# A decoder layer with a mixture of experts: expert rows in five tiles of 128 and one odd row, two groups per expert

## The reference

```
N, E, F = 4096 tokens, 8 experts, 512
capacity = int(N / E * 1.25) + 1                 # 641 rows for an expert
scores = softmax(xf @ wg); top1 = argmax(scores); combine_w = scores[top1]
rank = position of the token among those of its expert
slot = top1 * capacity + rank  (rank < capacity, else dropped)
eb = rows of xf by slot, 8 x 641 x 128           # empty slots are zero
y = gelu(eb @ W1 + b1) @ W2 + b2                 # 128 -> 512 -> 128
out = y[slot] * combine_w  (0 for a dropped token)
x = layernorm(x + out)
```

## Time and profile before

| what | value |
|---|---|
| time, median of 3 runs | 502.6 us (502.14 to 502.91) |
| profiled execution: its own time, and its span | 500.05 us, 498.1 us |
| busy in the span: PE, PEld, DVE, ACT, POOL | 88%, 61%, 68%, 58%, 58% |
| last work of the attention stage | about 381.7 us into the span |
| second layer of expert 0 starts; of expert 7 | 399.06 us; 472.16 us |

### The profile page before, as it was taken

How to read it: one execution, slowest core, us unless ns; L and a number is a source line. 1 busy time by engine, 2 the same in 40 slices (tenths; PEclk the granted TensorE clock), 3 DMA queues, 4 the chain that set the end, 5 groups by cost and what they waited for, 6 DMA issues and landing times.

```text
span 498.1 us, 18035 instructions
## 1 busy us (share of the span) xinstructions
PE 438.9 (88%) x6359; PEld 304.1 (61%) x6359; DVE 337.2 (68%) x1672; ACT 286.8 (58%) x627; POOL 290.7 (58%) x518
## 2 busy tenths in 40 slices
PE   3689999999999999999999999999861699999930
PEld 2355666666666666666666666666540488888730
DVE  5165677777787787777777777777774267767730
ACT  1256566766666776666676765676542256667620
POOL 5344555566566566566656666656444036887883
PEclk9999999999999999999999999999985599999985
DMA  4600000000111000011000010000004333344100
GB/s 148 227 13 12 24 14 17 24 25 24 29 34 30 24 24 24 25 35 33 25 24 24 24 37 17 19 13 19 15 29 120 84 81 89 101 107 128 26 19 18
DMA packets 30891, 22.51 MB, mean 45 GB/s; under 512 B 4460, under 2 KB 27281, under 8 KB 30804
## 3 DMA queue, kind: packets, MB, share of 16 engines
q1 hardware_dynamic: 27604, 17.16, 12.2%
q0 software_dynamic: 3200, 4.22, 2.8%
HBM read 12.25 MB, written 9.65 MB: 44 GB/s over the span
## 4 chain that ended last, share of the span: by engine, by line
PE 69%; issue 14%; POOL 9%; DMA 2%; DVE 1%; ACT 1%; SPq 1%; POOLq 1%; DVEq 0%; ACTq 0%
PE banks L529 14%; PE banks L591 13%; PE banks L537 9%; PE banks L545 8%; PE banks L523 6%; POOL out_x L480 6%; PE banks L602 6%; PE banks L670 3%; PE banks L618 3%; POOL rs L470 2%; PE banks L682 2%; PE banks L736 1%; PE banks L571 1%; PE banks L573 1%; PE banks L572 1%
## 5 line engine op out<-in xcount | busy, mean ns | idle before, releaser
L1001 DVE TENSOR_REDUCE mx<-banks 128x8 f32<-128x1024 f32 x64 | 75.4, 1219 | 12.4 <-PE banks L545 12.3
L417 POOL TENSOR_SCALAR QE<-qT,head_mask 128x128 f32<-128x128 f32 x128 | 75.6, 607 | 9.9 <-DVE qT L917 9.9
L806 ACT ACTIVATE arena<-banks 128x1024 f32<-128x1024 f32 x64 | 62.1, 1022 | 20.8 <-PE banks L545 20.8
L771 ACT ACTIVATE arena<-banks 128x1024 f32<-128x1024 f32 x64 | 62.1, 1023 | 18.0 <-PE banks L545 15.6
L591 PE MATMUL banks<-arena,V 128*32 128x128 f32 x2048 | 69.9, 276 | 1.2 <-ACT arena L806 0.7
L423 POOL TENSOR_TENSOR rs<-ve,minus_half 128x1 f32<-128x1 f32 x32 | 17.7, 552 | 84.4 <-DVE ve L971 84.4
L591 PEld LDWEIGHTS banks<-arena,V 128*32 128x32 f32 x2048 | 51.7, 109 | 12.6 <-issue 9.7
L480 POOL DMA_INDIRECT out_x<-ot,idx x48 | 49.9, 1040 | 12.1 <-issue 10.2
L434 POOL TENSOR_TENSOR rs<-ve,minus_half 128x1 f32<-128x1 f32 x32 | 18.1, 566 | 49.5 <-DVE ve L990 49.5
L818 ACT COPY yx<-banks 128x512 f32<-128x512 f32 x32 | 18.8, 586 | 48.9 <-PE banks L591 48.9
L545 PE MATMUL banks<-later,identb 64*64 64x256 bf16 (+1 forms) x448 | 46.3, 299 | 0.0
(11 more groups left out here) (150 smaller groups left out, 1004.7 us busy)
## 6 DMA issues: line engine op xcount, KB each, us to landing
w_sb<-in_L_ffn_W SPq DMA_DIRECT2D x16, 256.0 KB
expert_in<-zeros SPq DMA_DIRECT2D x10, 273.0 KB, 3.2
EB<-expert_in SPq DMA_DIRECT2D x8, 341.2 KB
X<-in_x SPq DMA_DIRECT2D x32, 64.0 KB, 1.8
C<-in_ctx SPq DMA_DIRECT2D x32, 64.0 KB, 1.9
out_x<-fb SPq DMA_DIRECT2D x32, 64.0 KB
out_x<-ot,idx POOLq DMA_INDIRECT x48
b2b<-in_L_ffn_b SPq DMA_DIRECT2D x1, 512.0 KB, 5.2
```

Of the source, the lines that this page charges most:

```text
L417: last = g.tensor_scalar(QE[b % 2][:, a, :], qT[b % 2][:], head_mask[:, a:a + 1], None, ALU.mult)
L771: nc.scalar.activation(A1[b % 2][:, 2 * half:2 * half + 2].rearrange("p j a t -> p j (a t)"), pair("s1", half), ACT.Relu).then_inc(s1_out[ ...
L806: nc.scalar.activation(P2[b % 2][:, 2 * half:2 * half + 2].rearrange("p j a t -> p j (a t)"), pair("s2t", half), ACT.Exp, scale=SCALE).the ...
L1001: v.tensor_reduce(mx[b % 2][:, 8 * half:8 * half + 8].rearrange("p (j a) -> p j a", a=NA), pair("s2", half).rearrange("p j (a t) -> p j a ...
```

## The change

The rows of an expert are five tiles of 128 (640 rows) and one odd row, the 641st. `ET` becomes 5, `CAPP` 656, and `JT = ET + 1` counts the tiles with the odd one. An expert's load now gives each partition five consecutive rows of the buffer (2600 bytes) where it gave six rows 112 apart (520 bytes each). The eight odd rows come with one small load (`ER`, 8 rows) and are transposed together once; each expert's hidden layer treats its odd row as column 641. In the second layer the odd row goes first: four matmuls with W2 as weights and one column moving. VectorE copies that column into `restY`; during expert 7 the eight columns are transposed back and finished as one tile of 8 rows. Each expert has two groups, tiles 0 to 2 and 3 to 4. `shifted` of the first group stands after `summed` of tile 4, that of the second after the next expert's `gated` and `token_rows`.

```diff
+    ET = CAP // P
+    JT = ET + 1
+    ROWS = ET * P + 1
+    HALVES = [(0, 321), (321, ROWS)]
+    CAPP = 656
...
+        GROUPS = [(e, tiles) for e in range(E) for tiles in ([0, 1, 2], [3, 4])]
...
             def expert_rows(e):
-                sp.dma_start(EB[e % 3][:], buf[e * CAPP:(e + 1) * CAPP, :].rearrange("(c p) d -> p c d", p=ER)).then_inc(
+                sp.dma_start(EB[e % 3][:], buf[e * CAPP:e * CAPP + ET * P, :].rearrange("(p c) d -> p c d", c=ET)).then_inc(
                     eb_in[e % 3], 16)
...
+            expert_rows(0)
+            sp.dma_start(ER[:], buf.rearrange("(e c) d -> e c d", c=CAPP)[:, ET * P, :]).then_inc(er_in, 16)
+            for e in range(1, 3):
                 expert_rows(e)
```

On GpSimd:

```diff
-            for n in range(GROUPS):
-                root(n)
-                if n >= LATE:
-                    scatter(n - LATE)
-            for n in range(GROUPS - LATE, GROUPS):
-                scatter(n)
+            for e in range(E):
+                if e > 0:
+                    scatter(2 * e - 1)
+                root(2 * e)
+                if e == E - 1:
+                    root_rest()
+                root(2 * e + 1)
+                scatter(2 * e)
+            scatter_rest()
+            scatter(2 * E - 1)
```

On TensorE, in `second_layer`:

```diff
-                for c in range(ET):
-                    n, rows = e * ET + c, tile_rows(c)
-                    if n >= 2:
-                        pe.wait_ge(y_done, n - 1)
+                for k in range(JT):
+                    i = e * JT + k
+                    if i >= 2:
+                        pe.wait_ge(y_done, i - 1)
                     for f in range(FC):
-                        mm = pe.matmul(max_bank[n % 2][0:rows, 0:D], hT[e % 2][:, f, c * ER:c * ER + rows],
-                                       w2_sb[e % 2][:, f, :], start=(f == 0), stop=(f == FC - 1))
+                        if k == 0:
+                            mm = pe.matmul(max_bank[i % 2][:, 0:1], w2_sb[e % 2][:, f, :], hT[e % 2][:, f, ET * P:ROWS],
+                                           start=(f == 0), stop=(f == FC - 1))
+                        else:
+                            mm = pe.matmul(max_bank[i % 2][:, 0:D], hT[e % 2][:, f, (k - 1) * P:k * P],
+                                           w2_sb[e % 2][:, f, :], start=(f == 0), stop=(f == FC - 1))
                     mm.then_inc(y_full, 1)
+                    if e == E - 1 and k == 2:
+                        pe.wait_ge(t_done, 2 * E)
+                        pe.transpose(dve_bank[0][0:E, 0:P], restY[:], ident[:]).then_inc(rest_full, 1)
```

On ScalarE, after the eight Gelus of expert e:

```diff
-                for n in range(max(0, (e - 1) * PER + 1), e * PER + 1):
-                    scaled(n)
+                if e > 0:
+                    scaled(2 * e - 1)
+                scaled(2 * e)
```

On VectorE:

```diff
+            for e in range(E):
+                if e > 0:
+                    spread_of(e - 1, ET - 1, stats(e - 1, ET - 1))
+                gate_mark = gated(e)
+                token_rows(e)
+                if e == 0:
+                    rest_mark = rest_gated()
                 else:
+                    shifted(2 * e - 1)
+                if e + 1 < E:
+                    rows_turned(e + 1)
+                rest_copied(e)
+                for c in range(ET):
+                    if c > 0:
+                        mark = stats(e, c - 1)
+                    summed(e, c, gate_mark)
+                    if c > 0:
+                        spread_of(e, c - 1, mark)
+                    if c == ET - 1:
+                        shifted(2 * e)
+                if e == E - 1:
+                    spread_of(e, ET - 1, stats(e, ET - 1))
+                    rest_summed(rest_mark)
+            dve.wait_ge(rstd_rest, 1)
...
```

More of the change, by code:

```diff
@@ L1 @@
+import math
 from contextlib import ExitStack
@@ L199, in decoder, with late @@
         w2_sb = ring("w2_sb", 2, [P, FC, D])
[L200 to L210, removed]
+        EB = ring("EB", 3, [P, ET, DR])
+        ER = sb("odd_rows", [E, DR])
+        b2r = sb("b2r", [E, D])
+        def late(at, shape):
+            size = math.prod(shape)
+            assert at + 2 * size <= 4 * SC
+            parts = [arena[:, at + k * size:at + (k + 1) * size] for k in range(2)]
+            if len(shape) == 2:
+                parts = [part.rearrange("p (a b) -> p a b", a=shape[0]) for part in parts]
+            return parts, at + 2 * size
+        ebT, end = late(0, [ROWS])
+        hT, end = late(end, [FC, ROWS])
+        xg, end = late(end, [ET, D])
         act_bank = [banks[:, k, :] for k in range(4)]
@@ L362, in _ @@
             for k in range(4):
-                sp.wait_ge(out_done[k], 16 * GT * (GROUPS // 4))
+                sp.wait_ge(out_done[k], 16 * sum(len(GROUPS[n][1]) for n in range(k, len(GROUPS), 4)))
+            sp.wait_ge(rest_out, 16)
         @block.gpsimd
@@ L465, in root @@
             def root(n):
-                e, c = n // PER, n % PER * GT
+                e, tiles = GROUPS[n]
+                c0, c1 = tiles[0], tiles[-1] + 1
                 pool.wait_ge(var3_ready, n + 1)
@@ L729, in first_layer @@
                 pe.wait_ge(w_in[e % 2], 32 * (e // 2 + 1))
-                rows = ebT[e % 2][:].rearrange("p c r -> p (c r)")
                 for f in range(FC):
-                    for half in range(2):
+                    for half, (r0, r1) in enumerate(HALVES):
                         j = 2 * FC * e + 2 * f + half
@@ L850, in scaled @@
             def scaled(n):
-                e = n // PER
+                e, tiles = GROUPS[n]
                 act.wait_ge(shift3_ready, n + 1)
[L854 to L861, removed]
+                before = [len(GROUPS[m][1]) for m in range(n % 4, n, 4)]
+                if before:
+                    act.wait_ge(out_done[n % 4], 16 * sum(before))
+                for t, c in enumerate(tiles):
+                    nc.scalar.activation(ot[n % 4][:, t, :], r3[e % 2][:, c, :], ACT.Identity,
+                                         bias=nm3[e % 2][:, c:c + 1],
+                                         scale=rs3[e % 2][:, c:c + 1]).then_inc(ot_ready, 1)
             for e in range(E):
                 for f in range(FC):
-                    for half in range(2):
+                    for half, (r0, r1) in enumerate(HALVES):
                         j = 2 * FC * e + 2 * f + half
@@ L1135, in rows_turned, with scatter_rows @@
             def rows_turned(e):
[L1136 to L1141, removed]
+                dve.wait_ge(t_full, 2 * e + 1)
+                if e >= 2:
+                    dve.wait_ge(h_full, 2 * FC * (e - 1))
+                v.tensor_copy(ebT[e % 2][:, 0:4 * P], dve_bank[0][:, 0:4 * P]).then_inc(t_done, 1)
+                dve.wait_ge(t_full, 2 * e + 2)
+                if e == 0:
+                    own.mark(v.tensor_copy(restT[:], dve_bank[1][:, P:P + E]))
+                    own.wait()
+                v.tensor_copy(ebT[e % 2][:, ET * P:ROWS], restT[:, e:e + 1])
+                v.tensor_copy(ebT[e % 2][:, 4 * P:ET * P], dve_bank[1][:, 0:P]).then_inc(t_done, 1)
+            def scatter_rows(to, left, token):
+                own.mark(v.tensor_scalar(left, token, 0.0, BIG, ALU.is_equal, ALU.mult))
+                own.wait()
+                return v.scalar_tensor_tensor(out=to, in0=token, scalar=-1.0, in1=left, op0=ALU.add, op1=ALU.add)
             def token_rows(e):
-                token = EB[e % 3][:, :, TOKEN]
-                own.mark(v.tensor_scalar(unfilled[:], token, 0.0, BIG, ALU.is_equal, ALU.mult))
-                own.wait()
                 for k in range(4):
-                    left = [n for n in range(GROUPS) if n % 4 == k and n // PER < e - 2]
+                    left = [len(tiles) for n, (of, tiles) in enumerate(GROUPS) if n % 4 == k and of < e - 2]
                     if left:
-                        dve.wait_ge(out_done[k], 16 * GT * len(left))
-                v.scalar_tensor_tensor(out=idx[e % 3][:], in0=token, scalar=-1.0, in1=unfilled[:],
-                                       op0=ALU.add, op1=ALU.add).then_inc(idx_ready, 1)
+                        dve.wait_ge(out_done[k], 16 * sum(left))
+                scatter_rows(idx[e % 3][:], unfilled[:], EB[e % 3][:, :, TOKEN]).then_inc(idx_ready, 1)
             def gated(e):
@@ L1223, in _, with rest_gated, rest_summed @@
-            spread_of(E * ET - 1, stats(E * ET - 1))
-            shifted(GROUPS - 1)
+            def rest_gated():
+                dve.wait_ge(er_in, 16)
+                scatter_rows(idxr[:], unfilledr[:], ER[:, TOKEN:TOKEN + 1])
+                return own.mark(v.scalar_tensor_tensor(out=xgr[:], in0=b2r[:], scalar=ER[:, GATE:GATE + 1],
+                                                       in1=ER[:, 0:D], op0=ALU.mult, op1=ALU.add))
+            def rest_summed(gate_mark):
+                dve.wait_ge(rest_full, 1)
+                own.wait(gate_mark)
+                own.mark(v.scalar_tensor_tensor(out=r3r[:], in0=dve_bank[0][0:E, 0:P], scalar=ER[:, GATE:GATE + 1],
```

(7 more changed lines are left out.)

159 lines of the change are left out of this document (75 added, 84 removed).

## The result

The changed kernel takes 506.7 us, the median of 4 runs (505.63 to 508.56); the kernel before took 502.4 beside it, the median of 4 (497.54 to 502.91). The ratio of the two kernels, which is estimated from all these runs and not from the two medians, is 1.0136, with a 95% interval of 1.0096 to 1.0175. In a later comparison it was 504.3 against 501.8, ratio 1.0071 (1.0038 to 1.0104). The changed kernel is slower, by about 1%.

What follows compares the result with a forecast made beforehand. TensorE was taken to set the expert stage's pace and GpSimd the tail. Start -0.2, seven periods +6.5 and tail -1.6 give +4.7 on the 502.6 median: 507.3 us, range 501.2 to 510.3.

Steps and rivals of the forecast that it cites:

- odd row, O: Second layer on TensorE: time of the odd row's four matmuls (eight records), taken as 0.88 us per expert.
- first Gelu after the second layer's start: ScalarE: the first Gelu waits behind three `scaled` until O + 6.84, 1.64 us after TensorE's result is ready.
- TensorE's wait before its fifth matmul: Sign in the first layer: TensorE idle near 0.8 us, having run four matmuls ahead, until the first Gelu ends.
- Gelus apart where data wait: ScalarE: Gelus of 529 ns can start 0.44 us apart, against TensorE's pace of 0.54.
- period without late results: Expert stage, from one second layer to the next: 0.88 + 10.49 = 11.37 us, against 10.44 before.
- from expert 7's second layer to the end: The tail, mostly GpSimd's roots and scatters: 24.3 us against 25.9, a gain of 1.6.
- The hold: ScalarE's queue: Gelus wait behind the first group's three `scaled`, delaying the next second layer by 0.92 us.
- 4-byte rows: Basis for O: one-column 4-byte records still cost the 128-column weight load, 0.11 us each, 0.88 for eight.
- nearly free: Rival on TensorE's odd column: O is 0.24 instead of 0.88, total 502.2, no change to be seen; chance 0.13.
- Gelus catch up: ScalarE: late Gelus close up to 0.44 us apart; the rival has them stay 0.54 apart, total 512.2, chance 0.08.
- The hold costs nothing: Rival on ScalarE: first group's `scaled` done by O + 5.2, so period 10.45 and total 500.9; chance 0.12.
- The start: Expert 0's rows: larger pieces land 0.5 us sooner, turning them costs 0.3 more, together -0.2 (-0.9 to +0.4).

Runs made afterwards that it cites:

- the groups of two and three: Changed kernel with the group border moved (tiles 0 to 1, then 2 to 4): ratio 0.9938 to the kernel before, 0.9950 when run again.

## Why the prediction was right

The forecast was 507.3 and slower; the result 506.7. By its steps, with the second profile of the changed kernel (span 502.4) beside the first. In the first, only expert 0 had no late result, so its values stand there. For the second those of later experts stand; expert 0's agree with the first profile's to 0.01:

| step | predicted | first profile | second profile |
|---|---|---|---|
| odd row, O | 0.88 | 0.92 | 0.92 |
| first Gelu after the second layer's start | 7.72 | 7.89 | 7.78 |
| TensorE's wait before its fifth matmul | near 0.8 | 0.66 | 0.56 |
| Gelus apart where data wait | 0.44 | 0.43 | 0.43 |
| period without late results | 11.37 | 11.49 | 11.39 |
| seven periods against before | +6.5 | +10.3 | +6.8 |
| start, less the attention stage's own shift | -0.2 | -0.3 | -0.6 |
| from expert 7's second layer to the end | 24.3 | 23.5 | 23.4 |

**The hold** was the mechanism that the runs confirmed from three sides: moved out of ScalarE's way it is gone, with the border moved it is gone, and put into the kernel before it appears. Its price, predicted as 0.92, measured 0.92 in expert 0 and 0.82 in the later ones. That the whole period came out within 0.02 of the forecast (11.39 for 11.37) is partly luck: the period without the hold, forecast as 10.45, is 10.57, and that error and the one in the hold nearly cancel.

**The odd row** fell on the side of the 4-byte rows, and the rival "nearly free" is refuted: eight records at 0.11. The Trainium skill's page "TensorE: Matmul & The Clock Gate", section "LDWEIGHTS", puts a load at the column count over 1.2, an estimate of 107 ns for 128 columns; the records here are 112 ns apart. The floor for 1 to 64 moving columns in its section "Back-to-back issue gap" does not show here: the records with one moving column are 112 ns apart too.

**Gelus catch up**: 3.55 for eight against 4.32; that rival is refuted. **The hold costs nothing** is refuted too.

**The start**: landing 0.7 faster (2.94 from issue to first transpose for 3.60), the turning 0.33 slower (2.40 for 2.07), both as forecast. Two parts that the forecast did not have nearly cancelled: the last attention scatter took 0.3 longer to land, and the time from the first layer to the second was 0.2 shorter.

**What the steps did not have.** The tiles of 128 rows are 0.89 apart, not 0.87; five make 0.1 a period. The tail was 0.8 shorter than forecast: the scatter of 8 rows took 0.91, not 1.1, and the time behind the last scatter fell from 6.85 to 6.28. And the late results cost 3.6 us in the profiled execution, for which the forecast was 504.8 and the time 508.6.

**Luck in the number.** The 0.6 between forecast and median is less than these runs can tell: the ratio 1.0136 makes the change 6.8 us, the medians make it 4.3, and the second comparison, +0.7%, makes it 3.6. The forecast of 4.7 stands among them. The 1 us that the prediction claimed to be able to tell was too fine: the intervals are 0.3 to 0.4% to each side.

## What to carry to other kernels

When tiles are grouped more coarsely, look at when the first group's result is complete and what stands behind its consumer in an in-order queue: here one tile later, one tile more and one tile less behind it turned 0.6 us of slack into a delay of 1.6, and saving instructions on three engines made the kernel slower. Where a group border can be placed, try the small group first. Do not count a one-column matmul as free: here, with 128 weight columns in 4-byte floats, it took as long as one with 128 columns moving.

## What the hardware showed that I had not expected

- Matmul records with 128 weight and 128 moving columns follow 0.112 apart (a tile of eight in 0.89), as do those with one moving column; those with 112 or 82 weight columns and 128 moving 0.109 (0.87).
- In the expert stage an indirect DMA of 82 rows holds GpSimd for 1.40, of 112 or 128 rows mostly 0.94 to 1.07, of 8 rows 0.91.
- In one execution of the groups of two and three VectorE's sum starts 0.31 us after TensorE's last record of the tile began, in another execution of the same program up to 1.1 us after; in the changed kernel's first profile it was up to 1.42. TensorE's granted clock was 1.00 there. No run here says why.
